# First attention of a two-layer model on one core: where the row sums of the softmax are made

## The reference, cut to what matters

```python
scores = jnp.einsum('bhqd,bhkd->bhqk', q, k) * scale
scores = scores + slopes[:, None, None] * dist[None, :, :].astype(jnp.float32)
...
scores = jnp.where(causal[None, None], neg_inf, scores)   # a window of 64 back
weights = jax.nn.softmax(scores.astype(jnp.float32), axis=-1)
out = jnp.einsum('bhqk,bhkd->bhqd', weights, v)
...
return out @ wo.T
```

## Time and profile before

| what | value |
|---|---|
| median of 3 runs | 2040.58 us (2039.21 to 2042.43) |
| the profiled execution | 2040.25 us, span 2038.5 us |
| the first attention's loop | 91 to 594 us of the span |
| a head without routing | 15.21 us from scores to scores |

### The profile page before, as it was taken

The page is one execution under the profiler, slowest core; times in us unless marked ns, Lnnn a source line. Parts: engine busy times, 40 slices in busy tenths (PEclk is TensorE's granted clock), DMA queues, the critical chain, the costliest instruction groups (busy, mean ns, idle before and its releaser), DMA issues. The chain is left out here.

```text
span 2038.5 us, 36208 instructions
## 1 busy us (share of the span) xinstructions
PE 1538.0 (75%) x12536; PEld 850.3 (42%) x12536; DVE 1315.1 (65%) x3285; ACT 1115.4 (55%) x2869; POOL 547.8 (27%) x614
## 2 busy tenths in 40 slices
PE   6799989999961999136999999999999735424910
PEld 3367666666641899121222222222222225323910
DVE  4554556656562422377999999999999277843423
ACT  3366666766640444241888888888888633101300
POOL 1133323625436300761001001001000020372056
PEclk8799999999995999565999999999999967556965
DMA  6144311111101775241000000000000000014832
GB/s 203 33 172 169 99 31 35 47 31 43 40 26 36 255 234 167 66 126 62 22 21 23 20 24 24 21 26 18 27 18 3 1 1 6 21 47 125 257 90 71
DMA packets 86208, 139.61 MB, mean 68 GB/s; under 512 B 18084, under 2 KB 57252, under 8 KB 85772
## 3 DMA queue, kind: packets, MB, share of 16 engines
q1 hardware_dynamic: 62860, 92.60, 15.6%
q0 software_dynamic: 11936, 34.49, 5.2%
q10 hardware_dynamic: 11232, 10.23, 1.5%
HBM read 76.03 MB, written 45.11 MB: 59 GB/s over the span
## 5 line engine op out<-in xcount | busy, mean ns | idle before, releaser
L2063 DVE TENSOR_REDUCE q_max<-s_ps 128x1 f32<-128x1024 f32 x512 | 598.0, 1218 | 14.0 <-PE s_ps L1954 6.4
L2044 ACT ACTIVATE probs<-s_ps 128x512 f32<-128x512 f32 x1024 | 535.5, 602 | 124.4 <-PE s_ps L1975 124.2
L1954 PE MATMUL s_ps<-k_stack,q_stack 64*128 64x512 bf16 x1024 | 351.4, 397 | 16.8 <-PEq L97 8.5
L1975 PE MATMUL s_ps<-q_stack,k_stack 64*128 64x512 bf16 x1024 | 319.5, 384 | 20.2 <-ACT probs L2044 15.8
L1989 PE MATMUL o_ps<-probs,v_aug 128*32 128x512 f32 x2048 | 273.6, 606 | 0.7 <-ACT probs L2044 0.7
L872 ACT ACTIVATE probs<-s_biased,s_min 128x128 f32<-128x128 f32 x512 | 199.3, 393 | 58.4 <-DVE s_min L961 57.0
L1975 PEld LDWEIGHTS s_ps<-q_stack,k_stack 64*128 64x128 bf16 x1024 | 78.4, 94 | 334.3 <-ACT probs L2044 282.5
L990 POOL TENSOR_TENSOR probs<-probs,p_rsum 128x512 f32<-128x512 f32 x128 | 133.1, 1040 | 305.8 <-DVE p_rsum L967 305.1
L1581 POOL CAST neg_max_parts<-neg_max 16x128 bf16<-16x128 f32 x32 | 9.0, 283 | 474.4 <-DVE neg_max L2071 474.4
L961 DVE CUSTOM_DVE_ANT_0 s_biased<-score_ps,nbias 128x128 f32<-128x128 f32 x512 | 117.7, 286 | 25.4 <-PE score_ps L738 21.5
L1954 PEld LDWEIGHTS s_ps<-k_stack,q_stack 64*128 64x128 bf16 x1024 | 77.3, 94 | 112.9 <-DVE q_max L2063 104.0
(11 more groups left out here) (313 smaller groups left out, 2741.4 us busy)
## 6 DMA issues: line engine op xcount, KB each, us to landing
moe0b_wblock<-in_L_ffn_blocks SPq DMA_DIRECT2D x39, 578.0 KB, 4.0
moe_rows<-zero_rows POOLq DMA_DIRECT2D x18, 960.0 KB, 4.5
moe1b_wblock<-in_L_ffn_blocks SPq DMA_DIRECT2D x39, 256.0 KB, 3.7
v_shift<-v_tiles SPq DMA_DIRECT2D x32, 256.0 KB, 3.1
v_shift<-v_tiles SPq DMA_DIRECT2D x32, 224.0 KB, 3.6
qk_parts_dram<-qk_parts SPq DMA_DIRECT2D x16, 384.0 KB, 2.7
q_stack<-qk_parts_dram SPq DMA_DIRECT2D x192, 32.0 KB
k_stack<-qk_parts_dram SPq DMA_DIRECT2D x192, 32.0 KB
```

The costliest lines, as they stand in the source:

```text
L1954: mm = nc.tensor.matmul(s1[u % 2][:, c * CH:(c + 1) * CH], qs[head_rows(m), quad % 4, j, qt * P:(qt + 1) * P], ks[head_rows(m), quad % 4, ...
L1975: nc.tensor.matmul(bank_of("exp", 4 * k + pos)[:], ks[head_rows(m), quad % 4, j, kt * P:(kt + 1) * P], qs[head_rows(m), quad % 4, j, half ...
L2044: nc.scalar.activation(pr[:, k % 2, HEADS[pos], :], bank_of("exp", n)[:], ACT.Exp).then_inc(sm["exp"], 1)
L2063: v.tensor_reduce(mx[:, h % 4, col:col + 1], s1[u % 2][:], AX.X, ALU.max).then_inc(sm["maxed"], 1)
```

## The change

The exponentials no longer write row sums. VectorE makes them in one pass over the group's four tiles, behind the wait for the exponentials and ahead of the reciprocal, with a semaphore of its own between the two:

```diff
         (h_in, p_mm, a_out, q_out, v_sh0, v_sh1, s_mm, biased, exped, rsum, normed, turned, pt_out, pv_mm, o_out,
-         wo_mm, wo_gated, x_added, scaled, shifted) = K.sems(
+         wo_mm, wo_gated, x_added, scaled, shifted, summed) = K.sems(
...
                             r = nc.scalar.activation(pr[:, g % 3, i, :], sb_[:, g % 2, i, :], ACT.Exp, scale=-1.0,
-                                                     bias=mn[:, g % 4, i:i + 1], accum_out=sm[:, g % 4, i:i + 1])
+                                                     bias=mn[:, g % 4, i:i + 1])
...
                     if 1 <= g < G + 1:
                         dve.wait_ge(exped, g)
+                        v.tensor_reduce(sm[:, (g - 1) % 4, :], pr[:, (g - 1) % 3], AX.X, ALU.add).then_inc(summed, 1)
+                        dve.wait_ge(summed, g)
                         v.reciprocal(ri[:, (g - 1) % 4, :], sm[:, (g - 1) % 4, :]).then_inc(rsum, 1)
```

More of the change, by code:

```diff
@@ L634, in window_attention_stage @@
         (h_in, p_mm, a_out, q_out, v_sh0, v_sh1, s_mm, biased, exped, rsum, normed, turned, pt_out, pv_mm, o_out,
-         wo_mm, wo_gated, x_added, scaled, shifted) = K.sems(
+         wo_mm, wo_gated, x_added, scaled, shifted, summed) = K.sems(
             st, "win", "h_in", "proj_mm", "act_out", "q_out", "v_shift_even", "v_shift_odd", "score_mm", "biased",
             "exp", "rsum", "normed", "turned", "probsT_out", "pv_mm", "o_out", "wo_mm", "wo_gated", "x_added",
-            "scaled", "shifted")
+            "scaled", "shifted", "summed")
         v_sh = (v_sh0, v_sh1)
```

## The result

The changed kernel takes 2049.81 us (median of 6 runs, 2047.47 to 2050.66) where the kernel before takes 2039.87 (6 runs, 2037.69 to 2042.43): the ratio is 1.0046, with a 95% interval of 1.0033 to 1.0059. It is slower by 9.9 us; 9.7 were forecast.

A forecast was written before the change was run, and what follows sets the result against it. TensorE's 41 us of standing still in the first attention's loop was taken as the bound. Losses of 18.2 us less a gain of 8.5 made 9.7 us longer, median 2050.3 us (0.48% slower), range 2038 to 2061.

The forecast's parts named there:

- The bound and the three waits: First attention, 91 to 594 us: TensorE's 41 us idle sets the end; waits for bias 18.2, `oT` 17.3, scaling 1.9 us.
- ScalarE's gain: Exponentials ahead of `oT`: four take 1.18 instead of 1.55 us; 0.37 at 20 places plus three at group 18, 8.5 us.
- The pass's price: VectorE's 128 row-sum reductions: 0.69 us each plus 0.04 to the reciprocal, 0.73 a pass; bounds 0.33 and 1.18.
- Plain heads hidden: Heads without routing pieces: the pass is hidden with 0.2 us to spare; a head takes 14.84 instead of 15.21 us.
- Routed groups: Groups where routing pieces used up the slack: the pass is not hidden; losses 18.2 us, or 25 passes of 0.73.
- the chains that go through VectorE alone: Routed groups, reciprocal to later scores: 0.73 at groups 16 to 18 and 28 to 30; 0.71 at scores 14.
- The waits for GpSimd's scaling: Routed groups: transposes wait another 0.36 at group 9, and 0.38 twice in groups 12 to 15.
- no gain at `oT`: Groups 12 to 15: of 1.67 us lost, 0.57 come back where L779 stood idle; net loss 1.10, group 15 without own gain.
- the transposes' wait: Groups 8 to 11: 1.2 us more, and transposes wait another 0.36 for GpSimd: 1.55 in second batch, 1.16 in later batches.
- The routed places together: Losses per routed batch before ScalarE's gain is taken off: second 4.56 us, third 5.20, fourth 8.47 including the loop's end.
- the prediction's chain: Loop's end, VectorE the bound: passes ahead of choice of experts, weights and placing, one more at last scaling; 4.0 us.

The follow-up runs named there:

- the dose: The changed kernel with each pass made twice, the first into a tile not read: 2092.5 us against 2042.4 for the kernel before, ratio 1.0247.
- the run that has the cost without the relief: The changed kernel with exponentials still writing their accumulators, into a tile not read: 2063.0 us against 2042.4 for the kernel before, ratio 1.0104.

## Why the prediction was right

**The bound and the three waits** were read rightly. The whole change of the time is in TensorE's idle time of this loop, and in its clock there.

**ScalarE's gain** was right in size: 1.19 us for four exponentials (forecast 1.18), 0.37 at each stall. Two stalls of L779 gave 0.65 instead of 0.37 (group 3 of the second batch, group 23 of the fourth): the waits of 0.91 and 1.09 there went to 0.25 and 0.44. One in the first batch gave 0.09. And group 15 of the three routed batches gave 0.30 each, where the forecast had no gain (below). Without any sums the kernel gained 9 to 11 us; 10.7 was expected.

**The pass's price** was right: 0.68 and 0.72 to the reciprocal. The estimate from the table in the errata section of the Trainium skill's page "VectorE: DVE Perf Modes", 0.59 us, is refuted by the 681 ns row. The same section says below its table that the measured fixed term is about 150 cycles and not 58. With that the estimate would be 0.69 us, which the row bears out.

**Plain heads hidden**: right, with 0.3 us to spare instead of 0.2; the dose shows that the second pass is no longer hidden.

**Routed groups**: the places were right (36 passes at them carry nearly the whole cost; only the 0.31 behind group 3 of the first batch is not in the forecast), and the chains that go through VectorE alone were right to 0.03 us (0.72 for 0.73 at groups 16 and 28; 0.72 for 0.71 at 13). The waits for GpSimd's scaling were right in size as well: in groups 11 and 15 the transposes start 1.93 us behind the scores in place of 1.59, which is 0.34 later where 0.36 and 0.38 were forecast. What was mis-sized is what L779, which comes next and stood waiting for `oT` itself, gives back. Group 15 of the second batch, before:

```profile
263.07 0.60 PE L750 MATMUL probsT_ps<-ident,probs 128*128 128x128 f32 x4
...
264.29 2.05 PE L779 MATMUL wo_ps<-woT_gated,oT 128*128 128x128 f32 x16 [0.62 <-ACT oT L880]
```

The same in the changed kernel, and in the run that keeps the reads:

```profile
264.43 0.66 PE L750 MATMUL probsT_ps<-ident,probs 128*128 128x128 f32 x4 [0.17 <-POOL probs L992]
...
264.93 1.95 PE L779 MATMUL wo_ps<-woT_gated,oT 128*128 128x128 f32 x16
```

```profile
267.09 0.66 PE L751 MATMUL probsT_ps<-ident,probs 128*128 128x128 f32 x4 [0.17 <-POOL probs L993]
...
267.79 2.05 PE L780 MATMUL wo_ps<-woT_gated,oT 128*128 128x128 f32 x16
```

From the group's scores (261.48, 262.50, 265.16) to L779 it is 2.81 us before, 2.43 in the changed kernel and 2.63 with the reads kept. With the reads kept the step is 0.18 shorter than before, just the 0.19 of the forecast (0.38 of waiting less the 0.57 given back); without them it is 0.49 shorter. So the step that failed is the forecast's "no gain at `oT`" here: the relief of ScalarE still gives 0.30 of its 0.37, in each of the three batches. At group 11 the forecast counted the transposes' wait in full, but L779 started 0.68 behind them before and starts 0.49 behind them now, so the step is only 0.05 longer (0.18 in the later batches). The routed places together were 0.6 us too high in the second batch (4.19 forecast, 3.59 measured) and 0.7 in the third (4.83 and 4.12).

**What was missing** is the clock. In the fourth batch a drop cost 0.95 us at group 18, and at the loop's end the step from scores 126 to 127 became 1.87 longer, of which the prediction's chain gives 0.72: about 1.15 for the second drop. This is an estimate; where groups 122 to 127 are those of the kernel before, the drop alone cost 1.38, and without any sums 1.28. Without the two drops the loop would be about 7.9 us longer in this profile, not 9.96. The direction, the places and the size of one pass are to the forecast's credit; that it hit 9.7 to 0.2 us is luck, since an overestimate of nearly 2 us and an omission were of one size. The medians may compare more evenly than the one pair of profiles does, since the kernel before has a drop in one of its two profiles; they give 9.9.

What stays open: why the drop at the loop's end is in every edited kernel and in neither profile of the kernel before. It came even where groups 122 to 127 are unchanged and the stall ahead of it, at scores 126, is as long as before (1.97 us against 1.96), so a longer stall there is not needed for it. Two profiles are few, and no run here set it apart.

## What to carry to other kernels

Moving work to an engine with more idle time is not priced by that idle time. List the stalls of the bounding engine by the group in which they occur, and ask of each group which instruction is ahead of the one waited for: here 33 of 128 groups held nearly all of the gain, 36 others nearly all of the cost, and choosing per group turned 0.46% slower into 0.50% faster. When a schedule is regular, subtract two traces step by step; the sum of a profile can be right for wrong reasons more easily than its steps. A step can mislead as well: at group 15 only the run that has the cost without the relief told a smaller loss from a larger gain.

## What was not expected of the hardware

TensorE's granted clock fell from full to half, for a few microseconds at a time (0.50 in each of the three microseconds behind scores 18 of the fourth batch in the changed kernel), in the middle of a loop in which it is over 90% busy (462 of 503 us before). The drops inside the loop came behind the stall at group 18, which lasts 1.85 to 3.05 us in these runs, and in the last groups, where stalls follow each other; and the same kernel showed 1.00 in one execution and 0.64 over 6 us in another. Most cost 0.6 to 1.7 us (2.2 at one place with two passes), beside the 9.9 us that were being measured.
